# Attention with its projections: the low parts of the first step's probabilities on VectorE instead of the last step's, and the next input's splits in other slots

## The reference

```python
x = ft.reshape(B, N, C)                                  # 16, 1024, 512
qkv = (x @ w_qkv + b_qkv).reshape(B, N, 8, 3 * 64)
q, k, v = jnp.split(qkv, 3, axis=-1)
attn = jnp.einsum('bxhd,byhd->bxyh', q, k) * 64 ** -0.5
attn = jax.nn.softmax(attn, axis=2)
res = jnp.einsum('bxyh,byhd->bxhd', attn, v).reshape(B, N, 512)
res = res @ w_out + b_out + x
```

## Time and profile before

| | us |
|---|---|
| median of 3 runs (3841.31 to 3845.83) | 3842.76 |
| the profiled execution's own time | 3843.17 |
| its span in the profile | 3841.1 |
| TensorE busy, matmuls | 3784.3 (99%) |
| weight loads of TensorE | 3084.5 (80%) |
| VectorE / ScalarE / GpSimd busy | 2720.4 / 3018.9 / 1982.5 |

### The profile page before, as it was taken

One profiled execution on the slowest core, in us unless ns is written; L12 is line 12 of the kernel. 1 busy time (PEld: TensorE's weight loads), 2 busy tenths in 40 slices (PEclk: granted clock), 3 DMA queues, 4 the chain that ended last, 5 costly groups with the idle time before them and its releaser, 6 DMA issues.

```text
span 3841.1 us, 93450 instructions
## 1 busy us (share of the span) xinstructions
PE 3784.3 (99%) x37132; PEld 3084.5 (80%) x37132; DVE 2720.4 (71%) x4643; ACT 3018.9 (79%) x5141; POOL 1982.5 (52%) x1022
## 2 busy tenths in 40 slices
PE   7999999999999999999999999999999999999998
PEld 5878888888888888888888888888888888888886
DVE  6776767777676776767767677676776767767775
ACT  6887878878787787877878788787887877878786
POOL 2464644546445464454645546455454544646444
PEclk9999999999999999999999999999999999999999
DMA  3011111212102121021211211112111111111101
GB/s 94 21 54 45 56 45 26 59 40 56 48 23 67 35 56 48 21 72 29 56 48 33 66 26 54 48 40 62 26 54 48 48 54 26 53 48 43 51 23 56
DMA packets 100709, 178.26 MB, mean 46 GB/s; under 512 B 16192, under 2 KB 16192, under 8 KB 100288
## 3 DMA queue, kind: packets, MB, share of 16 engines
q1 hardware_dynamic: 100288, 172.29, 16.2%
HBM read 71.57 MB, written 33.55 MB: 27 GB/s over the span
## 4 chain that ended last, share of the span: by engine, by line
PE 90%; issue 3%; ACT 3%; POOL 2%; DVE 2%; DMA 0%; SPq 0%; ACTq 0%; DVEq 0%
PE psum L573 36%; PE psum L592 13%; PE psum L624 11%; PE psum L626 11%; PE psum L649 5%; PE psum L651 4%; PE psum L650 4%; PE psum L654 3%; PE psum L653 1%; PE psum L582 1%; POOL xT_lo L483 1%; POOL p_lo L489 1%; ACT p_hi L733 1%; PE psum L600 1%; ACT k_lo_hi L717 1%
## 5 line engine op out<-in xcount | busy, mean ns | idle before, releaser
L489 POOL TENSOR_TENSOR p_lo<-p_full,p_hi 128x1024 f16<-128x1024 f32 x768 | 1646.9, 2145 | 1727.1 <-ACT p_hi L733 1725.4
L732 ACT ACTIVATE p_full<-psum,prob_bias 128x512 f32<-128x512 f32 x2048 | 1428.2, 697 | 575.7 <-PE psum L626 565.5
L833 DVE TENSOR_REDUCE max_parts<-psum 128x1 f32<-128x512 f32 x2048 | 1372.2, 684 | 543.8 <-PE psum L592 543.6
L733 ACT ACTIVATE p_hi<-psum,prob_bias 128x512 f16<-128x512 f32 x2048 | 1425.0, 696 | 0.0
L592 PE MATMUL psum<-k_lo_hi,q_hi_hi 128*128 128x512 f32 x2048 | 857.2, 439 | 13.5 <-DMA q_hi_hi<-q_hi_hi 5.5
L624 PE MATMUL psum<-q_hi_hi,k_lo_hi 128*128 128x512 f32 x2048 | 804.4, 393 | 5.2 <-DVE q_shift L843 3.7
L626 PE MATMUL psum<-q_shift,k_shift 128*128 128x512 f32 x2048 | 802.6, 392 | 0.0
L649 PEld LDWEIGHTS psum<-v_parts,p_hi 128*128 128x128 f16 x6144 | 568.0, 98 | 278.4 <-issue 221.6
L649 PE MATMUL psum<-v_parts,p_hi 128*128 128x65 f16 x6144 | 764.8, 194 | 11.4 <-POOL p_lo L489 11.4
L650 PE MATMUL psum<-v_parts,p_hi 128*128 128x64 f16 x6144 | 756.2, 193 | 0.0
L651 PE MATMUL psum<-v_parts,p_lo 128*128 128x65 f16 x6144 | 752.7, 194 | 0.0
(11 more groups left out here) (71 smaller groups left out, 5871.3 us busy)
## 6 DMA issues: line engine op xcount, KB each, us to landing
q_hi_hi<-q_hi_hi SPq DMA_DIRECT2D x256, 128.0 KB, 2.2
k_shift<-k_lo_hi SPq DMA_DIRECT2D x256, 128.0 KB, 2.2
y_tile<-in_x SPq DMA_DIRECT2D x125, 256.0 KB, 2.7
result<-y_tile SPq DMA_DIRECT2D x125, 256.0 KB, 2.0
x_in<-in_xT SPq DMA_DIRECT2D x121, 256.0 KB, 2.9
o_heads<-in_L_conv_w_qkv SPq DMA_DIRECT2D x12, 256.0 KB, 4.2
p_full<-in_xT SPq DMA_DIRECT2D x4, 256.0 KB, 5.2
o_heads<-in_L_conv_w_out SPq DMA_DIRECT2D x4, 256.0 KB, 3.2
```

The lines of the kernel that those rows point to most:

```text
L489: nc.gpsimd.tensor_tensor(p_lo[:, g % LO_SLOTS, :, :], p_full[:, g % 2, :, :], p_hi[:, g % HI_SLOTS, :, :], ALU.subtract).then_inc(p_lo_re ...
L732: nc.scalar.activation(p_full[:, g % 2, n, :], scores(g, n), ACT.Exp, scale=SCALE, bias=prob_bias[:, :])
L733: nc.scalar.activation(p_hi[:, g % HI_SLOTS, n, :], scores(g, n), ACT.Exp, scale=SCALE, bias=prob_bias[:, :]).then_inc(exp_done, 1)
L833: nc.vector.reduce_max(max_parts[:, u % 2, q_tile, k_half:k_half + 1], bank(b, w), AX.X).then_inc(done["row_max"], 1)
```

## The change

Two tables are changed. `POOL_STEPS` gives GpSimd steps 1, 2, 3 of each unit and VectorE step 0, where GpSimd had 0, 1, 2 and VectorE 3. `X_SPLIT_SLOT` moves three of the eight splits: part 2 from slot -17 to -16, part 6 from -13 to -12, part 7 from -11 to -12.

```diff
-X_SPLIT_SLOT = (-18, -17, -17, -16, -14, -13, -13, -11)
+X_SPLIT_SLOT = (-18, -17, -16, -16, -14, -13, -12, -12)
 O_TRANSPOSE_SLOT = (62, 64, 65, 67, 68, 69, 70, 72)
...
-POOL_STEPS = (0, 1, 2, 4, 5, 6)
+POOL_STEPS = (1, 2, 3, 5, 6, 7)
 
 
 def on_pool(s):
     return s % 8 in POOL_STEPS
```

## The result

The changed kernel takes 3930.87 us (median of 4 runs, 3930.02 to 3931.68) against 3843.2: 1.0227 times the time before, 95% interval 1.0214 to 1.0240. The forecast was 3911 us with a range of its own of 3900 to 3923, and 3880 to 3940 with its rivals.

A forecast was written before the change was run, and what follows sets the result against it. TensorE was taken to bound the kernel, almost never waiting. Holds of 0.77, 0.19, 0.24, 1.07, 1.23 and 1.16 less 0.34 make 4.32 us per image; fifteen images plus the last, 68 us, give 3911 us, own range 3900 to 3923.

The forecast's parts named there:

- the rival with the tight units: Rival, chance 0.17: step 16 and units like it hold too, if the need is 2.1 to 2.2 us; 24 us more, 3935.
- TensorE sets the time, a new wait is paid in full: TensorE almost never waits, so any new mid-stream wait adds its full length unless a later wait would have taken it.
- The place of the wait: Step 0's low part on VectorE delays the reduction of tile 3, whose bank TensorE wants for tile 5.
- The price of 1.98 us from ScalarE's end to tile 5: Time a unit needs from ScalarE's end of its step 0 to tile 5: start, low part, reduction, 0.14 us signal.
- the holds at 0, 8 and 40: TensorE's waits before tile 5 in the units beginning at these steps: 0.77, 0.19 and 0.24 us per image.
- Step 48 with the wait for GpSimd, 1.23: VectorE's low part waits for GpSimd's x part 1; tile 5 follows GpSimd's end by 1.82 us, a hold of 1.23 us.
- Step 52, 1.16: VectorE's low part waits for GpSimd's x part 5, ending at 2123.8; TensorE held 1.16 us before tile 5.
- a gain at 49 and 50: TensorE's wait for GpSimd's low part of step 49 shrinks, saving at most 0.34 us before `k_lo` takes over.
- The ten units with no hold: The other ten of sixteen units have enough room before tile 5; step 16 is tightest, 2.00 us for 1.98; cost 0.
- The first image at the price of the others: First image counted at 4.32 us like the others, despite less room in some units; error up to 3 us.
- GpSimd's longer low part of the last step: 0 to 0.1: GpSimd's low part of step 3 takes 2.15 us instead of 1.23; tightest at step 43; at most 0.1 us per image.
- no port wait: Rival, chance 0.17: VectorE doesn't wait for GpSimd's x part; holds at steps 48 and 52 are 0.74 and 0.38; 3892 us.

The follow-up runs named there:

- experiment 3: The changed kernel with VectorE's `step_lo` written after the loop over the late row-max tiles, behind the reduction of tile 3; 3952.68 us, 1.0282.
- experiment 6: The changed kernel with the fifth row-max tile (tile 5) moved from the early to the late place of its slot; 3862.99 us, 1.0049.
- Experiment 5: The changed kernel with one bias addition in slot 57 instead of 56, x part 1 split a slot earlier, parts 5 and 7 a slot later; 3894.88 us, 1.0133.
- experiment 4: The changed kernel with one bias addition on GpSimd in slot 57 instead of 56; 3919.93 us, 1.0198.
- all remedies together: The changed kernel with tile 5 late, one bias addition in slot 57, x part 1 split a slot earlier, parts 5 and 7 later; 3857.70 us, 1.0038.

## Why the prediction was right, and where it was short

The place and the kind of the wait were right, the size was 20 us short. The measured time lies outside the forecast's own range (3900 to 3923); it lies in the whole range because the rival with the tight units had stretched that to 3940, and that rival's cause was wrong. This much of the hit is luck.

- *TensorE sets the time, a new wait is paid in full.* Right. The holds of the ninth image add up to its loss, and none of them comes back later. The Trainium skill (Perfetto Trace Analysis, Identifying the Most-Contended Engine) has TensorE's headroom judged by its share of peak arithmetic and by the share of its weight loads; the prediction read 80% as a fifth free and set the starts against it. The starts were right: a load takes 188 ns (the row of L592 above) and a matmul of 512 columns starts every 0.23 us, so some 80% is what a full engine shows in this kernel.
- *The place of the wait: the reduction of tile 3 behind step 0's low part, tile 5's bank.* Right: the rows of step 44 show it, experiment 3 moves the wait to another tile, and experiment 6 takes most of it away.
- *The price of 1.98 us from ScalarE's end to tile 5.* Measured 1.91. The signal from the reduction to tile 5 took 0.06 us and not 0.14. The 0.14 was misread: in the kernel before the reduction of tile 3 ends 0.13 or 0.14 us before tile 5 at nearly all sixteen units of the image, also at step 4, where it starts 2.3 us behind ScalarE's end. So it was TensorE's own pace, TensorE did not yet wait there, and some 0.08 us were to spare. But after a real wait the matmul behind tile 5 starts 0.34 us after it (2146.12 to 2146.46 at step 44) and not 0.25 as before. The two errors cancel: the holds at 0, 8 and 40 came within 0.02 us and 43 and 44 together within 0.03. That they are so close is luck in part.
- *Step 48 with the wait for GpSimd, 1.23.* Right to 0.01 (with the figures of the recorded line the holds come to 1.20 and 1.15, and with 1.82 unrounded to 1.22 and 1.17, not 1.23 and 1.16; it changes nothing). Experiment 5, where 48 and 47 lose 0.72 together, shows that 0.5 us of it is this wait, and L852's 1.69 us for 1.23 says the same. The Trainium skill (SBUF — State Buffer, SBUF: two separate sides, on the shared port pair) states it as a lock for the whole instruction; L852 of 1.94 and 2.12 us agree.
- *Step 52, 1.16.* Short by 0.33. The term for GpSimd's queue failed: I took its times as they stand before. They follow the exponentials of step 50, which come behind the whole hold of step 48 (GpSimd's low part of step 50 is at 2167.53, in the kernel before at 2116.99, 50.54 us earlier), while TensorE had got 0.36 back by then. What I booked as a gain at 49 and 50 was taken away at 52. Experiment 5 shows the sum of it: with GpSimd free step 52 loses 0.24.
- *The ten units with no hold.* Nine of them had none. The "hair" of 0.02 us at step 16 was more than that by the measured need of 1.91. Step 56 failed: 0.71 us. Its room was enough, but GpSimd's bias addition, which had stood behind step 56's own low part, now starts right before VectorE's. The step of the prediction that failed is the list of what GpSimd has beside `step_lo`: I counted the splits and left out the additions (L496), so this term was put at nothing. 15 x 0.71 = 11 us; experiment 4 gives 10.9.
- *The first image at the price of the others.* 9.4 us instead of 4.3, where the forecast had allowed for an error of up to 3; it is 4.0 more than the others lose. The units at 4, 8, 12, 36 and 40 lose 0.8 to 1.1 us each. The room was there to be read in the trace of the kernel before: in the first image 0.92, 0.86 and 0.91 us at steps 4, 12 and 36, with no output projection of an earlier image in front of tile 5, in the second 3.16, 2.57 and 2.34 us, with 12, 6 and 6 of their matmuls.
- *GpSimd's longer low part of the last step: 0 to 0.1.* 0.11 at step 43. TensorE is later by that when it comes to tile 4, so the hold at 44 is smaller by about as much.

Together: 68 us, and 11 (step 56), 5 (step 52) and 4 (the first image, beyond what the others lose) give the measured 88. The last image lost 3.2 us for a forecast of 3.3. The rival "no port wait" is wrong, and so is "the tight units hold too" as I put it: the extra loss has their size and another cause.

Left open: how much of the 14 us that stay with all remedies together comes from the remedies themselves (tile 5's late place, two splits in slot 46).

## What to carry to other kernels

When an operation moves in a queue, look for what the saturated engine wants back first from behind it: the time from the operation's last input to that return, against the time until the engine asks for it, both read from two rows per place, gave five holds within 0.03 us (43 and 44 taken as one), by luck in part, as said above. List everything that a neighbour which blocks the operation does in the new time, not only what the change names: a bias addition cost 11 us. And a gain on one engine is only kept if the others' queues move up with it.

## What the runs showed of the hardware

VectorE's `step_lo` (L852, both inputs in SBUF) and GpSimd's `tensor_tensor` of a split or a bias addition (L483, L496) hold each other up. VectorE's took 1.23 us alone, and 1.69, 1.94 and 2.12 us when GpSimd's operation of 1.29 us had started 0.68, 0.44 and 0.25 us earlier: lead and duration add up to 2.37 or 2.38 us each time, for a split (0.68, 0.44, 0.25) as for a bias addition (0.44). Both wait in turn at step 48 of the changed kernel:
```profile
2158.14 1.29 POOL L483 TENSOR_TENSOR xT_lo<-x_in,xT_hi 128x512 fp32r<-128x512 f32 x1
...
2158.82 1.69 DVE L852 TENSOR_TENSOR p_lo<-p_full,p_hi 128x1024 f16<-128x1024 f32 x1 [0.68 <-ACT p_hi L733]
...
2159.38 2.25 POOL L483 TENSOR_TENSOR xT_lo<-x_in,xT_hi 128x512 fp32r<-128x512 f32 x1
```

x part 1 ends at 2159.43, VectorE's operation 1.08 us later, and the next x part, which starts at 2159.38, is held up by VectorE in its turn and takes 2.25 us. In each pair the one that is held up shows this as its own duration and not as idle time (the 0.68 us before L852 are its wait for ScalarE), so a list of waits doesn't name it; the spread of an operation's durations does.
